# Two routed-expert stages: experts taken in pairs, with 64-column gate and up products, 64-row down products and w_down in 6144-byte rows

## The reference

```python
E, K, H, F = (64, 6, 512, 192)          # experts, experts per token, channels, hidden width
CAP = 2 * (T * K // E)                  # 96 slots per expert
buf = jnp.zeros((E, CAP + 1, H), x.dtype).at[se, slot].set(x[tok])[:, :CAP]
h = jax.nn.silu(jnp.einsum('ech,ehf->ecf', buf, w_gate)) * jnp.einsum('ech,ehf->ecf', buf, w_up)
out = jnp.einsum('ecf,efh->ech', h, w_down)
gathered = out[se, jnp.minimum(pos, CAP - 1)] * valid.astype(x.dtype)[:, None]
return jax.ops.segment_sum(gathered * w, tok, num_segments=Tn)
```

## Time and profile before

| | us |
|---|---|
| median of 3 runs | 1491.81 |
| lowest and highest run | 1488.98, 1502.8 |
| span of the profiled execution | 1489.4 |
| TensorE busy in it | 1323.8 (89%) |
| VectorE, ScalarE, GpSimd busy | 640.1, 550.0, 508.2 |

### The profile page before, as it was taken

One profiled execution on the slowest core, in us unless ns is written; L12 is line 12 of the kernel. 1 busy time (PEld: TensorE's weight loads), 2 busy tenths in 40 slices (PEclk: granted clock), 3 DMA queues, 4 the chain that ended last, 5 costly groups with the idle time before them and its releaser, 6 DMA issues.

```text
span 1489.4 us, 21599 instructions
## 1 busy us (share of the span) xinstructions
PE 1323.8 (89%) x7858; PEld 810.4 (54%) x7858; DVE 640.1 (43%) x1300; ACT 550.0 (37%) x1265; POOL 508.2 (34%) x413
## 2 busy tenths in 40 slices
PE   4999999999992688999999899989998999999990
PEld 4633776766761444654564464445434776766660
DVE  6774222222224466555654754532683222222220
ACT  1311111111111178776876886763211111111110
POOL 0022355544542742232222322200031454555544
PEclk9797999999995788999999999979995999999995
DMA  8985799999988644232542343221845899999986
GB/s 307 391 311 169 232 310 314 313 314 303 308 225 243 203 115 124 72 81 65 134 106 72 100 99 86 72 72 50 282 149 170 253 311 311 307 313 310 313 212 125
DMA packets 164618, 307.08 MB, mean 206 GB/s; under 512 B 19617, under 2 KB 52769, under 8 KB 164513
## 3 DMA queue, kind: packets, MB, share of 16 engines
q1 hardware_dynamic: 131136, 238.07, 50.6%
q0 software_dynamic: 23808, 57.69, 17.1%
q10 hardware_dynamic: 9568, 9.94, 2.0%
HBM read 222.54 MB, written 61.87 MB: 191 GB/s over the span
## 4 chain that ended last, share of the span: by engine, by line
PE 59%; DMA 15%; DVE 10%; issue 6%; ACT 4%; POOL 4%; SPq 1%; DVEq 0%; POOLq 0%; ACTq 0%
DMA buf<-xn_d,tok 11%; PE ps L388 9%; PE ps L447 6%; PE ps L503 5%; PE ps L405 5%; PE ps L491 4%; PE ps L392 4%; PE ps L514 4%; PE ps L409 3%; PE ps L459 3%; PE ps L432 3%; PE ps L373 2%; PE ps L284 2%; PE ps L276 1%; ACT ps L697 1%
## 5 line engine op out<-in xcount | busy, mean ns | idle before, releaser
L388 PE MATMUL ps<-bufT,gu 128*128 128x96 f32 x2048 | 254.8, 279 | 0.0
L388 PEld LDWEIGHTS ps<-bufT,gu 128*128 128x128 f32 x2048 | 243.7, 195 | 1.8 <-issue 1.6
L1163 POOL DMA_INDIRECT buf<-xn_d,tok x128 | 128.0, 1000 | 286.6 <-DVE osb L994 219.0
L1063 DVE TENSOR_REDUCE Mx<-ps 128x1 f32<-128x512 f32 x256 | 168.5, 684 | 101.9 <-PE ps L459 101.3
L987 DVE TENSOR_TENSOR h<-sg,ps 128x96 f32<-128x96 f32 x128 | 32.6, 254 | 405.2 <-ACT sg L663 279.7
L697 ACT ACTIVATE ps<-ps,Mx 128x512 f32<-128x512 f32 x256 | 171.6, 671 | 43.2 <-DVE Mx L1063 38.7
L723 ACT ACTIVATE PT<-ps 128x512 f32<-128x512 f32 x256 | 153.1, 605 | 66.2 <-PE ps L491 64.8
L663 ACT ACTIVATE sg<-ps 128x192 f32<-128x192 f32 x128 | 42.4, 331 | 336.5 <-PE ps L392 333.4
L405 PE MATMUL ps<-wd,h 128*96 128x512 f32 x256 | 125.3, 612 | 2.2 <-DVE hr L988 2.2
L491 PE MATMUL ps<-St 98*128 98x512 f32 x256 | 120.2, 480 | 6.6 <-ACT PT L723 6.5
L1205 POOL TENSOR_TENSOR t<-t,rp 128x512 f32<-128x512 f32 x32 | 41.1, 1285 | 247.6 <-DVE t L1048 246.7
(11 more groups left out here) (152 smaller groups left out, 1713.4 us busy)
## 6 DMA issues: line engine op xcount, KB each, us to landing
gu<-in_L_ffn_w_gate SPq DMA_DIRECT2D x64, 768.0 KB
gu<-in_L_ffn_w_up SPq DMA_DIRECT2D x64, 768.0 KB
wd<-in_L_ffn_w_down SPq DMA_DIRECT2D x64, 512.0 KB
St<-HL SPq DMA_DIRECT2D x192, 128.0 KB, 2.3
wr<-in_L_ffn_w_down SPq DMA_DIRECT2D x128, 128.0 KB
wqk<-wp_d SPq DMA_DIRECT2D x32, 512.0 KB, 5.5
xn_d<-XN SPq DMA_DIRECT2D x24, 256.0 KB, 2.1
X<-in_L_attn_X SPq DMA_DIRECT2D x4, 1024.0 KB, 10.8
```

The source lines that it names most:

```text
L388: e.matmul(bk[:, CAP * j:CAP * j + CAP], w[:, c, 0:128], f.bufT[x % 3][:, c, :], start=(c == 0), stop=(c == 3))
L1063: e.tensor_reduce(Mx[:, qt, hl:hl + 1], bank((4, 5, 7)[n % 3]), AX, ALU.max, negate=True).then_inc(a_max, 1)
L1163: e.indirect_dma_start(out=f.buf[x % NB][:, :], out_offset=None, in_=f.xn_d, in_offset=bass.IndirectOffsetOnAxis(ap=f.tok[:, x:x + 1], axi ...
```

## The change

The step of `pe_experts` becomes a pair: step `st` of 34 turns both experts of pair `st`, then does gate and up of pair `st - 1`, then down of pair `st - 2`. Gate and up are cut into three strided sets of 64 columns (`j:F:3`), and each product of one expert runs in one column half while the same product of the other expert runs in the other half. Down is cut into three blocks of 64 hidden rows with the two experts in the two row halves. Hidden unit 3p+j sits at partition p and block j, and so w_down is loaded as one transfer with 6144-byte rows in place of three transfers with 2048-byte rows. ScalarE applies silu once per pair, VectorE forms h once per pair. `bufT` has four tiles in place of three. `gather`, `pool_experts` and the number of `buf` tiles are untouched.

```diff
-                f.ring = [(at("gu", g * KB, [128, 4, 4, F]), at("wd", d * KB, [128, 2, D]), at("wr", (d + 4) * KB, [128, D]))
+                f.ring = [(at("gu", g * KB, [128, 4, 4, F]), at("wd", d * KB, [128, 3, D])) for g, d in ring_at]
...
+        def pe_turned(e, f, x):
+            e.wait_ge(s_buf[f.n][x % NB], 16 * (x // NB + 1))
+            if x >= 2:
+                e.wait_ge(f_bTs, 64 * f.n + x - 1)
+            else:
+                e.wait_ge(f_shc, 16 * f.n + NT)
+            for c in range(4):
+                t = e.transpose(bank(x % 2)[:, CAP * c:CAP * c + CAP], f.buf[x % NB][:, 128 * c:128 * c + 128],
+                                cst[0:CAP, C_ID:C_ID + CAP])
+            t.then_inc(f_bT, 1)
+
+        def pe_gate_up(e, f, q):
+            gu = f.ring[q % NR][0]
+            e.wait_ge(f_bTs, 64 * f.n + 2 * q + 2)
+            e.wait_ge(s_gu[q % NR], loaded(f, 2 * q, 2))
+            if q >= 2:
+                e.wait_ge(f_h, 32 * f.n + q - 1)
...
+            for m in range(2):
+                bk = ps[1 + q % 2 * 2][:, m, :]
+                for j in range(3):
+                    for c in range(4):
+                        for k in range(2):
+                            t = e.matmul(bk[64 * k:64 * k + 64, CAP * j:CAP * j + CAP], gu[:, 2 * k + m, c, j:F:3],
+                                         f.bufT[(2 * q + k) % 4][:, c, :], start=(c == 0), stop=(c == 3),
+                                         tile_position=(0, 64 * k), skip_group_check=True)
+                t.then_inc(f_gu, 1)
+
+        def pe_down(e, f, q):
...
+            e.wait_ge(f_h, 32 * f.n + q + 1)
...
+            for j in range(3):
+                for k in range(2):
+                    p = slice(64 * k, 64 * k + 64)
+                    t = e.matmul(bank(4 + k)[0:CAP, :], f.h[q % 2][p, CAP * j:CAP * j + CAP], wd[p, j, :], start=(j == 0),
+                                 stop=(j == 2), tile_position=(64 * k, 0), skip_group_check=True)
+                    if j == 2:
+                        t.then_inc(f_d, 1)
+
         def pe_experts(e, f):
...
+            for st in range(E // 2 + 2):
+                if st < E // 2:
+                    for x in (2 * st, 2 * st + 1):
+                        pe_turned(e, f, x)
+                if 0 <= st - 1 < E // 2:
+                    pe_gate_up(e, f, st - 1)
+                if st >= 2:
+                    pe_down(e, f, st - 2)
...
         def dve_experts(e, f):
...
+            for q in range(E // 2 + 1):
+                if q < E // 2:
...
+                    e.wait_ge(f_gu, 64 * f.n + 2 * q + 2)
+                    e.wait_ge(f_sg, 32 * f.n + q + 1)
+                    e.tensor_tensor(f.h[q % 2][:, :], f.sg[q % 2][:, :], ps[1 + q % 2 * 2][:, 1, 0:3 * CAP], ALU.mult).then_inc(f_h, 1)
+                if q:
+                    for x in (2 * q - 2, 2 * q - 1):
                         e.wait_ge(f_d, 64 * f.n + x + 1)
                         if x >= 4:
                             scattered(e, f, x - 4)
...
-            e.dma_start(wd[:, :, :], w_down[x, 0:128, :].rearrange("x p h -> p x h")).then_inc(s_dn[q % NR], 16)
-            for k in range(2):
-                e.dma_start(wr[64 * k:64 * k + 64, :], w_down[2 * q + k, 128:F, :]).then_inc(s_dn[q % NR], 16)
+            e.dma_start(wd[:, :, :], w_down[x].rearrange("x (p j) h -> (x p) j h", j=3)).then_inc(s_dn[q % NR], 16)
```

More of the change, by code:

```diff
@@ L205, in __init__ @@
                 o = A1 + NB * 2304
[L206 to L213, removed]
+                f.bufT = [at("bufT", o + j * 1536, [128, 4, CAP]) for j in range(4)]
+                o += 4 * 1536
+                f.sg = [at("sg", o + j * 1152, [128, 3 * CAP]) for j in range(2)]
+                o += 2 * 1152
+                f.h = [at("h", o + j * 1152, [128, 3 * CAP]) for j in range(2)]
+                o += 2 * 1152
                 f.osb = [at("osb", o + j * 2048, [CAP, D]) for j in range(4)]
@@ L361, in pe_route @@
                 pe_shared_down(e, f, 3)
-        def pe_experts(e, f):
[L364 to L403, removed]
-                    for k in range(2):
[L405 to L410, removed]
@@ new lines, in pe_down @@
+        def pe_down(e, f, q):
+            wd = f.ring[q % NR][1]
+            e.wait_ge(f_h, 32 * f.n + q + 1)
+            e.wait_ge(s_dn[q % NR], loaded(f, 2 * q, 1))
+            if q:
+                e.wait_ge(f_ev, 64 * f.n + 2 * q)
+            else:
+                e.wait_ge(f_tokd, 2 * f.n + 2)
+            for j in range(3):
[5 more added lines that the diff above has]
+                        t.then_inc(f_d, 1)
@@ L978, in dve_experts @@
         def dve_experts(e, f):
[L979 to L985, removed]
-                    e.wait_ge(f_sg, 64 * f.n + x + 1)
-                    e.tensor_tensor(f.h[x % 4][:, :], f.sg[x % 3][:, 0, :], bk[:, 2 * CAP:3 * CAP], ALU.mult)
-                    e.tensor_tensor(f.hr[x // 2 % 2][own, :], f.sg[x % 3][own, 1, :], bk[other, CAP:2 * CAP], ALU.mult).then_inc(f_h, 1)
-                if st % 2 and st >= 3:
-                    for x in (st - 3, st - 2):
+            for q in range(E // 2 + 1):
+                if q < E // 2:
+                    if q >= 2:
+                        e.wait_ge(f_d, 64 * f.n + 2 * (q - 2) + 2)
+                    e.wait_ge(f_gu, 64 * f.n + 2 * q + 2)
+                    e.wait_ge(f_sg, 32 * f.n + q + 1)
+                    e.tensor_tensor(f.h[q % 2][:, :], f.sg[q % 2][:, :], ps[1 + q % 2 * 2][:, 1, 0:3 * CAP], ALU.mult).then_inc(f_h, 1)
+                if q:
+                    for x in (2 * q - 2, 2 * q - 1):
                         e.wait_ge(f_d, 64 * f.n + x + 1)
@@ L1262, in load @@
         def load(e, f, q):
-            gu, wd, wr = f.ring[q % NR]
+            gu, wd = f.ring[q % NR]
             x = slice(2 * q, 2 * q + 2)
```

31 lines of the change are left out of this document (15 added, 16 removed).

## The result

| | before | after |
|---|---|---|
| median, us | 1491.82 | 2109.91 |
| lowest and highest run | 1488.98, 1502.8 | 2105.67, 2114.08 |
| span of the profiled execution | 1489.4 | 2107.9 |
| TensorE busy in it | 1323.8 (89%) | 1397.6 (66%) |

The changed kernel takes 1.4135 times as long, 95% interval 1.4074 to 1.4197. The forecast was slower, 2276 us, with a range of 2110 to 2480. Direction and mechanism were right.

A forecast was written before the change was run, and what follows sets the result against it. TensorE was taken as the bound, busy 96% of the expert stages. Rounds of 23.1 us, 29 per stage plus ends, gave 700.5 us a stage, +784.6 in all: 2276 us, range 2110 to 2480.

The forecast's parts named there:

- The order (the deciding step): Transposes of pair q+3 directly follow down of pair q; gather cover falls from 9.13 us to 0, exposing 12.2 us.
- The sum: Expert-stage round from down to down: 12.2 + 0.9 + 6.9 + 3.1 = 23.1 us, paid 29 times per stage.
- Landing: Second gather's time from start until seen as landed: 7.5 us, between 3.77 without loads and 8.44 beside queued loads.
- The clock: TensorE falls to 1.2 GHz in each wait and returns 4.5 us into gate and up, making that 6.9 us.
- The edit to gate and up: Gate and up per pair: 96 64-column instructions take 4.86 us at full clock instead of 5.20, a change of -0.34 us.
- The rule of the Trainium skill: Gate and up: weight loads overlap only across row groups; 96 in series take 13.2 us, time some 2760; chance 1%.
- The clock that stays low throughout: Rival: TensorE stays at low clock through the whole burst, 28.2 us a round, 2572 us; 10%.
- the halves that do not overlap: Rival: gate and up's column halves don't run side by side, taking twice as long; 28.0 us a round, 2560; 3%.
- The third: Rival: the gather lands nearly unhindered, 4.67 + 3.77, giving 19.3 us a round and 2056 us; 8%.
- The other side: Rival: the gather wait stays hidden, 287 us a stage, 1450 us if the DMA also keeps up; 4%.
- two points of decision: Conditions for a hidden wait: eight buf tiles, or an eviction that does not read buf; neither found in the diff.
- What the profile was to show: DMA buf leading the chain at 58 rounds, TensorE busy about 65%, clock 0.6 to 0.7, DMA about 140 GB/s, attention unchanged.

The follow-up runs named there:

- the early release: Changed kernel with the weight column copied out of buf behind the transposes, gathers waiting for that copy and issued ahead of the scatters: 1475.83 us, 0.9885 of before.
- The two runs without loads beside them: Changed kernel without weight loads from pair 6 on, 1992.89 us; changed kernel with each ring load issued behind the round's transposes, 1989.15 us.
- the paired gathers: Changed kernel with GpSimd issuing both gathers of a pair ahead of the pair's two scatters: 2102.68 us.
- the 1463 reached at best: Changed kernel with buf released early and w_down loaded as three transfers of 2048-byte rows: 1462.95 us, 0.9788 of before.
- nine filling products: Changed kernel with nine thrown-away 128 x 512 products ahead of each pair's transposes from the fourth pair on: 2062.54 us.
- twelve: Changed kernel with ten thrown-away products ahead of the first transposes and two between the transposes of the two experts: 2020.57 us.

## Where the prediction was right, and the step that failed

*The order (the deciding step)* was right. The cover of a gather fell to nothing, the wait is paid 29 times per stage, the chain has an eviction, a scatter and a gather in each round. The old kernel with four tiles, the changed one with eight, and the one with the early release show it from three sides. That order, and not a product, is the loss.

*The step that failed* is the sum of a round: the second gather's landing, put at 7.5 us, measured 6.2, and gate and up after the wait, put at 6.9, measured 6.0. With the smaller terms below the forecast was 166 us too high. All four errors of the round, and the cheaper last rounds of each stage, went the same way. That the median then missed the range by only 0.1 us is chance; its executions, 2105.67 to 2114.08, lie on both sides of 2110.

*The sum* was 23.1 us a round. It measured 20.5. By terms:

| term | forecast | measured |
|---|---|---|
| down product's end to second gather | 4.67 | 4.55 |
| landing | 7.5 | 6.2 |
| transposes | 0.9 | 0.90 |
| gate and up | 6.9 | 6.0 |
| down | 3.1 | 2.80 |

23.1 - 20.5 is 2.6 us, times 58 is 151, and 2276 - 151 = 2125. The last 15 are the end of each stage: the ring has nothing left to load there, and the last three rounds take 17.6, 17.3 and 18.9 us, 7.7 less than three of 20.5, in both stages.

*Landing, the term that failed most.* I took 7.5, next to the 7.68 of a gather beside fresh loads, and called the 3.77 of no loads an unlikely bound. In the timeline above the first gather does land 7.35 us after its start, but the second starts 3.05 us later and takes 1.1 us less: the same loads are further on by then. I had given that 0.2 us. The two runs without loads beside them land in 3.8. So this landing behaves less like a latency than like the end of the burst: started 1.7 us earlier, it ends only 0.4 earlier (the paired gathers). The DMA view of the changed kernel, 255 to 270 us in 40 slices, shows the burst:

```profile
DMA  0000064899999999999998999999999700100000
GB/s 0 0 0 0 0 156 172 279 385 393 418 401 418 385 418 415 385 402 414 315 311 242 311 296 284 273 219 273 358 264 220 126 11 0 44 0 0 0 0 0
...
wd<-in_L_ffn_w_down SPq DMA_DIRECT2D x1, 768.0 KB, 8.3
```

The engines are full from 258 to 266.6 us, at about 400 GB/s while only loads move and at 220 to 360 once gathers and scatters are among them, from 261.5 on, and then they are nearly empty. The last load, issued at 257.33, lands at 265.6, the second gather at 266.8. 3.2 MB at the 311 GB/s of the earlier trace rows are 10.3 us, which from +0.9, where packets begin to move, ends at +11.2; it measured +10.8. Bytes and rate stood in the prediction; the +0.9 is read from this trace. Together they give the second gather's landing as an estimate of 6.5, where a duration copied from another place gave 7.5.

*The clock.* That it falls in each wait was right. It comes back earlier than the 4.5 us that I took; the windows of the round above show it:

```profile
270.00:271.00 1.00, 1.00 (x18) 1.00 (x16) 0.00 (x0) 0.00 (x0) 0.00 (x0) 0.50 0.00 0
271.00:272.00 1.00, 1.00 (x24) 1.00 (x24) 0.00 (x0) 0.33 (x1) 0.00 (x0) 0.84 0.00 0
```

(0.84 - 0.5) / 0.5 is 0.7 us at full clock, so it rose at 271.3, 3.6 us after gate and up had begun. The rest of that term is the product itself: 96 instructions at full clock take 4.42 us, and not the 4.86 that sixteen in 0.81 gave. Down likewise came out as three full products' worth, 2.80, just under the lower bound of 2.85.

*The edit to gate and up* was worth more than forecast, 5.20 to 4.42 us per pair where 4.86 was forecast, and a pair at full clock is 8.0 us and not 8.9 (rounds of the early release). Strided weights and different moving operands cost nothing, as said.

*The rule of the Trainium skill* (TensorE: Matmul & The Clock Gate, The mechanism) that loads overlap only across row groups would have made gate and up over 13 us. The same section also names a load into the background weight buffer as one that is pulled ahead, which I had left out. The trace disagrees with the rule as I used it: 96 loads and 96 products in 4.42 us, where 96 loads of 138 ns would be 13.2 in series.

*The rivals.* The clock that stays low throughout and the halves that do not overlap did not come. The third, a landing nearly unhindered, came in part: 6.2 lies between my 7.5 and its 3.8, and the time came between 2276 and 2056. I gave it 8% as if it were all or nothing. As a continuous term, with a bound of 3.77 that a row showed, it should have carried the range down to about 2050. The other side, a hidden wait, is what the early release made of it, and its 1450 was close to the 1463 reached at best. Of its two points of decision the eviction that does not read `buf` was right. Eight tiles are not enough: they give one pair of cover, about 8 us, where 11.8 are needed, and 1570 us.

*What the profile was to show:* DMA buf has 16% of the chain, TensorE busy 66% (65 forecast), granted clock 0.75 in a stage (0.6 to 0.7), DMA 142 GB/s (140). The stretch of attention, forecast as unchanged, came 8 us longer, and the part ahead of the first stage 9 us shorter. From run to run of this study these two varied by as much (692.6 to 703.3 us, and first transposes at 134.9 to 149.9 us).

## What to carry to other kernels

When steps are merged, count for each recycled buffer what lies between the instruction that frees it and the one that waits for its refill, in program order of the engine that waits; compare that with eviction, issue and landing together. Here it fell from 9.13 us to 0 while the number of tiles stayed the same, and a gain of one microsecond per pair in the products became a loss of ten. With the cover restored another bound came up at once, the scatters at 9.2 us a pair, and behind them the loads. The cure that gave most was to free the buffer when its last large reader is done, and let the small late reader have a copy.

## What the runs showed of the hardware that I had not expected

- Three kernels with different waits (the changed one, its version with paired gathers, the old one with four tiles) have median rounds of 20.5, 20.4 and 20.4 us, while the versions without loads in the wait have 18.05. With paired gathers the second transposes start 0.4 us earlier, and gate and up take 0.2 to 0.3 us longer, which takes most of it back.
- Behind fresh loads the first packet of GpSimd's queue moves 4.15 to 4.36 us after the first gather's issue, and 1.7 us after it where the loads come later. So 2.5 of the 3.7 us by which that gather is seen as landed later (7.0 against 3.3) pass before any of its bytes move.
- With nine filling products the array idled only 0.5 and 1.6 us in the round shown, and the clock still fell in most rounds: gate and up took 5.5 to 6.0 us in 43 of 58 and 4.4 in 15. With twelve it fell in none.
- A gather that waits for the first of two evictions starts after the second: evictions from 255.99 to 257.40, the gather at 257.52, 0.8 us after the first had ended; here and in the earlier trace rows. Over all such pairs of both kernels the gather starts 0.79 us after its own eviction and 0.13 us after the second (medians). GpSimd's issue seems to be held while VectorE evicts; this was seen, not tried.
- In a full queue, the accumulating scatters land 0.5 us later beside one w_down transfer of 6144-byte rows than beside three of 2048-byte rows (8.4 against 7.9 in the median), at 325 and 322 GB/s.
- With eight tiles gate and up take 6.8 us in the median at a granted clock of 0.99, and 4.5 with early release. This stays open.
